# A four-layer graph network: where the eight tile transposes of the third layer stand among the gather matmuls

## The chip, the cores and the metric

The kernel runs on one core of one Trainium2 chip. The metric is the device time of one execution in microseconds (us), the median of a few runs. On the core work five engines that this text names as the profile does: PE (TensorE, matmuls; its weight loads are shown apart as PEld), DVE (VectorE), ACT (ScalarE), POOL (GpSimd) and SP (SyncE, which here only issues transfers). They run side by side and meet at semaphores.

## The reference, cut to what matters

Four layers over 4096 nodes with 64 features and one 4096 x 4096 weighted adjacency matrix. Each layer normalises its input, aggregates over neighbours and adds to x. The change touches the third layer only (index 2), a hyperbolic one:

```python
def _logmap(x, y, c):
    sub = _mobius_add(-x, y, c)
    sub_norm = jnp.maximum(jnp.linalg.norm(sub, axis=-1, keepdims=True), MIN_NORM)
    ...
    arg = jnp.clip(sqrt_c * sub_norm, 0.0, TANH_CLIP)
    return 2.0 / (sqrt_c * lam_x) * jnp.arctanh(arg) * sub / sub_norm

deg = jnp.maximum(adj.sum(axis=1, keepdims=True), 1e-08)
log_ij = _logmap(x[:, None, :], x[None, :, :], c)
agg = jnp.einsum('ij,ijc->ic', adj / deg, log_ij)
```

So for every pair (i, j) there is one scalar, a function of the distance of the two nodes, which is symmetric in i and j; it is multiplied by adj[i, j] and the product gathers the features of j into i.

## The kernel before

**Units.** The third layer walks over the upper half of the pair matrix. A strip S is 512 nodes wide (eight strips), a pair p is 2 x 128 nodes. A unit is one (S, p) block of 256 x 512 scalars, held as 128 x 1024. Strip S has the units p = 2S to 15, so there are 16 + 14 + ... + 2 = 72 units. The first two units of a strip lie on the diagonal; the other units, 56 of them, are "mirrored": since the scalar is symmetric, their transpose serves the block below the diagonal too.

**The chain of one unit n**, in the order in which its data flow:

1. PE, `scores2` (L648): two fp32 matmuls (4 records of 512 columns) into one of two pairs of PSUM banks (0-1 or 2-3).
2. ACT, square (L879) of those banks into SBUF; then PE, `sides2` (two bf16 matmuls of 512 columns, shown under L452) adds a second term into the same banks.
3. DVE, `rest2` (L1235); ACT, Ln (L885), Exp (L891), Exp (L892), called `roots2`.
4. DVE, `sum2` (L1241), which needs the Exp of L891 and the sides; ACT, Ln (L896), called `arc2`; DVE, `pair2` (L1247). The result, the matrix of scalars, is in `sum_`, which has three buffers. It signals pair_ready.
5. POOL (L415) multiplies `sum_` with the near adjacency tile in place and signals near_ready.
6. Mirrored units only: PE, `mirror2` (L671), eight 128 x 128 fp32 transposes of `sum_` into PSUM banks 4-5; it signals mirror_ready. DVE, `far2` (L1253), multiplies those banks with the far adjacency tile and signals far_ready.
7. PE, `gather2_near` (fp32, shown under L452): two matmuls of 512 columns, 4 records, into bank 6, where it accumulates over the strip; `gather2_far`: four matmuls of 256 columns, 8 records, into bank 7. DVE, `far2_out` (L1261 or L1263), takes bank 7 out for each mirrored unit and signals far_out; `near2_out` (L1271 or L1274) takes bank 6 out once a strip.

**The order of PE.** It is written out by hand. In step n PE does `scores2(n+1)`, `sides2(n)`, `mirror2(n-1)`, `gather2_near(n-2)`, `gather2_far(n-2)`, each where it exists. So three units are in flight. Before `mirror2(n-1)` it waits for pair_ready of n-1 and for far_ready of the mirrored unit before, which has to have left banks 4-5.

**The order of DVE**, also by hand, in its iteration n: `far2_out(n-3)`, `near2_out(n-3)` where a strip ends, `sum2(n)`, `far2(n-1)`, `rest2(n+1)`, `pair2(n)`. ACT: `roots2(n)`, square(n+1), `arc2(n)`. Each engine does its work strictly in this order.

**SP** loads near and far tiles five units ahead into a ring (the fifth buffer is the tensor H), as soon as the gathers of the unit that had the buffer are done. Both kernels leave this alone.

The diff touches the loop of PE around L700 and the loop of DVE at its end.

Of the kernel before, what the change touches and what calls it, by code (L numbers as in the profile page):

```python
# [21 lines left out]
D = 64  # L22
P = 128
T = N // P
BANK = 512
# [19 lines left out]
ST = STRIP // P  # L45
NS = N // STRIP
PAIR = 2 * P
RING2 = 5
ROT = 2
ROTS = 3  # L50

UNITS = [(S, p) for S in range(NS) for p in range(2 * S, T // 2)]
NU = len(UNITS)


def mirrored(n):
    S, p = UNITS[n]
    return p >= 2 * S + 2


def mirrors(n):

    return sum(mirrored(m) for m in range(n + 1))
# [6 lines left out]
def closes(n):  # L70
    return n == NU - 1 or UNITS[n + 1][0] != UNITS[n][0]
# [11 lines left out]
def graph_layers(nc, x, adj_t, codes, w0_t, b0, w1_t, b1, wq_t, bq, wk_t, bk, scalars, w2, b2, w3, b3, out):  # L83
    ctx = ExitStack()
    with ctx:
        def sb(name, shape, dt=F32):
            return ctx.enter_context(nc.sbuf_tensor(name, shape, dt))
# [3 lines left out]
        def sem(name):  # L91
            if name not in named:
                named[name] = ctx.enter_context(nc.semaphore(name))
            return named[name]
# [9 lines left out]
        PS = ctx.enter_context(nc.psum_tensor("PS", [P, 8 * BANK], F32))  # L104
# [7 lines left out]
        ident = sb("ident", [P, P])  # L112
# [36 lines left out]
        def banks(a, b):  # L149
            return PS[:, a * BANK:b * BANK]  # L150
# [15 lines left out]
        def units_of(first, n):  # L166
            return work[:, first * UNIT:(first + n) * UNIT].rearrange("p (k n) -> p k n", k=n)
        root, lnr, sum_ = units_of(0, ROT), units_of(2, ROT), units_of(4, ROTS)
        GA = work[:, 7 * UNIT:11 * UNIT]
        Zn = work[:, 11 * UNIT:11 * UNIT + T * ROWS].rearrange("p (t c) -> p t c", t=T)  # L170
# [4 lines left out]
        def near(n):  # L175
            k = n % RING2
            return ring[:, k, 0:UNIT] if k < RING else Hflat[:, 0:UNIT]

        def far(n):
            k = n % RING2  # L180
            return ring[:, k, UNIT:2 * UNIT] if k < RING else Hflat[:, UNIT:2 * UNIT]

        def z_banks(n):
            return banks(ROT * (n % ROT), ROT * (n % ROT) + 2)
# [14 lines left out]
        def agg2_col(t):  # L199

            g, t = t // TG, t % TG
            return (2 + 3 * g + t // 7) * BANK + (t % 7) * (D + 1)
# [244 lines left out]
        def _(pe):  # L447
            mm = nc.tensor.matmul

            def add(out_ap, lhsT, rhs, starts=False):  # L450

                return mm(out_ap, lhsT, rhs, start=starts, stop=True, skip_group_check=True)  # L452
# [184 lines left out]
            def scores2(n):  # L637
                S, p = UNITS[n]
                if n == 0:
                    pe.wait_ge(sem("zr_out_a"), 1)  # L640
                    pe.wait_ge(sem("zl_out_a"), 1)
                if n == 2:
                    pe.wait_ge(sem("zr_out_v"), 1)
                    pe.wait_ge(sem("zl_out_v"), 1)
                if n >= ROT:
                    pe.wait_ge(sem("sum_ready"), n - ROT + 1)
                for q in range(2):
                    ins = mm(z_banks(n)[:, q * BANK:(q + 1) * BANK], TA[0:D + 1, (2 * p + q) * P:(2 * p + q + 1) * P],  # L648
                             TB[0:D + 1, S * STRIP:(S + 1) * STRIP], start=True, stop=True)
                ins.then_inc(sem("z_ready"), 1)  # L650

            def sides2(n):
                S, p = UNITS[n]
                pe.wait_ge(sem("square_ready"), n + 1)
                if n == 0:
                    pe.wait_ge(sem("kap_ready"), 4)
                for q in range(2):
                    ins = add(z_banks(n)[:, q * BANK:(q + 1) * BANK], kap_l[0:ROWS, (2 * p + q) * P:(2 * p + q + 1) * P],
                              kap_r[0:ROWS, S * STRIP:(S + 1) * STRIP])
                ins.then_inc(sem("side_ready"), 1)  # L660

            def mirror2(n):
                pe.wait_ge(sem("pair_ready"), n + 1)
                if n == 2:
                    pe.wait_ge(sem("zr_out_v"), 1)
                if mirrors(n) > 1:
                    pe.wait_ge(sem("far_ready"), mirrors(n) - 1)
                for i in range(ST):
                    for q in range(2):
                        c = 4 * BANK + i * PAIR + q * P  # L670
                        ins = nc.tensor.transpose(PS[:, c:c + P], sum_[:, n % ROTS, q * BANK + i * P:q * BANK + (i + 1) * P], ident[:, :])  # L671
                ins.then_inc(sem("mirror_ready"), 1)

            def gather2_near(n):
                S, p = UNITS[n]
                pe.wait_ge(sem("near_ready"), n + 1)
                if opens(n) and n:
                    pe.wait_ge(sem("near_out"), S)
                for q in range(2):
                    ins = add(PS[0:D + 1, 6 * BANK:7 * BANK], Zn[:, 2 * p + q, 0:D + 1], near(n)[:, q * BANK:(q + 1) * BANK],  # L680
                              opens(n) and q == 0)
                ins.then_inc(sem("agg2_near"), 1)

            def gather2_far(n):
                S, p = UNITS[n]
                pe.wait_ge(sem("far_ready"), mirrors(n))
                if mirrors(n) > 1:
                    pe.wait_ge(sem("far_out"), mirrors(n) - 1)
                for i in range(ST):
                    ins = add(PS[0:D + 1, 7 * BANK:7 * BANK + PAIR], Zn[:, S * ST + i, 0:D + 1], far(n)[:, i * PAIR:(i + 1) * PAIR], i == 0)  # L690
                ins.then_inc(sem("agg2_far"), 1)

            def nodes2(first, end):
                for t in range(first, end):
                    ins = mm(PS[:, agg2_col(t):agg2_col(t) + D + 1], GA[0:D + 1, t * P:(t + 1) * P], ident[0:D + 1, 0:D + 1],  # L695
                             start=True, stop=True)
                ins.then_inc(sem("agg2_nodes"), 1)

            scores2(0)
            for n in range(NU + 2):  # L700
                if n + 1 < NU:
                    scores2(n + 1)
                if n < NU:
                    sides2(n)
                if 1 <= n <= NU and mirrored(n - 1):
                    mirror2(n - 1)
                if n >= 2:
                    gather2_near(n - 2)
                    if mirrored(n - 2):
                        gather2_far(n - 2)  # L710
# [247 lines left out]
        def _(dve):  # L958
# [279 lines left out]
            def sum2(n):  # L1238
                dve.wait_ge(sem("root_ready"), n + 1)
                dve.wait_ge(sem("side_ready"), n + 1)  # L1240
                V.scalar_tensor_tensor(sum_[:, n % ROTS, :], z_banks(n), 1.0, sum_[:, n % ROTS, :], ALU.max, ALU.add)\  # L1241
                 .then_inc(sem("sum_ready"), 1)

            def pair2(n):
                dve.wait_ge(sem("tau_ready"), n + 1)
                dve.wait_ge(sem("rin_ready"), n + 1)
                V.scalar_tensor_tensor(sum_[:, n % ROTS, :], sum_[:, n % ROTS, :], TAU_MAX, lnr[:, n % ROT, :], ALU.min, ALU.mult)\  # L1247
                 .then_inc(sem("pair_ready"), 1)

            def far2(n):  # L1250
                dve.wait_ge(sem("mirror_ready"), mirrors(n))
                dve.wait_ge(sem(f"far_loaded{n % RING2}"), 16 * sum(mirrored(m) for m in range(n % RING2, n + 1, RING2)))
                V.tensor_tensor(far(n), banks(4, 6), far(n), ALU.mult).then_inc(sem("far_ready"), 1)  # L1253

            def far2_out(n):
                S, p = UNITS[n]
                at = GA[0:D + 1, p * PAIR:(p + 1) * PAIR]
                got = PS[0:D + 1, 7 * BANK:7 * BANK + PAIR]
                dve.wait_ge(sem("agg2_far"), mirrors(n))
                if S == 0:  # L1260
                    V.tensor_copy(at, got).then_inc(sem("far_out"), 1)  # L1261
                else:
                    V.tensor_tensor(at, at, got, ALU.add).then_inc(sem("far_out"), 1)  # L1263
# [13 lines left out]
            for n in range(NU + 3):  # L1277
                if n >= 3 and mirrored(n - 3):
                    far2_out(n - 3)
                if n >= 3 and closes(n - 3):  # L1280
                    near2_out(n - 3)
                if n < NU:
                    sum2(n)
                if 1 <= n <= NU and mirrored(n - 1):
                    far2(n - 1)
                if n + 1 < NU:
                    rest2(n + 1)
                if n < NU:
                    pair2(n)

            link(V.reciprocal(agg_y[:, :], deg[:, :]))
            link(V.tensor_tensor(agg_y[:, :], agg_y[:, :], iball[:, :], ALU.mult))
# [105 lines left out]
```

## Time and profile before

| what | value |
|---|---|
| median of 3 runs | 1236.74 us (1235.92 to 1241.49) |
| the profiled execution, its own time | 1238.63 us |
| its span in the trace | 1236.9 us, so 1.7 us lie around it |
| PE busy | 1100.3 us, 89% of the span |
| DVE busy | 857.2 us, 69% |
| ACT busy | 767.2 us, 62% |
| POOL busy | 371.0 us, 30% |
| third layer, the unit loop | about 630 to 1079 us of the span |

A line of a timeline gives the start of a group of like instructions, the time from the first start to the last end, engine, line and operation, output and input, shapes, their count, and in brackets the idle time before it with what ended that. Matmuls overlap: the record of one lasts past the start of the next, so what a group occupies on PE is read from its start to the start of the next group. An fp32 matmul is two records. "PEclk" is the share of the full TensorE clock that was granted.

### The profile page before, as it was taken

To read this page: it belongs to the slowest core of one execution; us is meant where nothing else is said; L and a number is where in the kernel's file an instruction comes from. 1 tells how busy PE (TensorE), PEld (TensorE's weight loads), DVE (VectorE), ACT (ScalarE), POOL (GpSimd) and SP (SyncE) were. 2 spreads that over 40 slices of the span, in tenths; PEclk is the share of its full clock that TensorE was granted. 3 is DMA by queue.
4 is the path that set the end of the run, shared out by engine and by line. 5 is a ranking of instruction groups with operands and counts; after the bars stand their busy time and mean duration, and the time that the engine had idled before them with its cause. 6 is when DMAs were issued, how large, how long until landed. Compare 5 with 4: busy or idle time off the path is not lost.

```text
span 1236.9 us, 15886 instructions
## 1 busy us (share of the span) xinstructions
PE 1100.3 (89%) x5064; PEld 495.1 (40%) x5084; DVE 857.2 (69%) x916; ACT 767.2 (62%) x780; POOL 371.0 (30%) x279
## 2 busy tenths in 40 slices
PE   2799999997599999999349999999999999954997
PEld 0233333347422222222124554554545454443555
DVE  7799989964766666666746777677677777666553
ACT  2355555543556656666338778778787888634864
POOL 6434334320100000000154334334333434323533
PEclk9899999996799999999768999999999999966999
DMA  8899999950067887776303446446454545111653
GB/s 321 282 349 366 341 338 354 343 205 1 1 229 260 265 267 268 266 261 219 136 1 121 156 133 192 158 127 202 138 170 136 179 131 163 52 55 43 194 185 89
DMA packets 96285, 237.97 MB, mean 192 GB/s; under 512 B 16368, under 2 KB 45040, under 8 KB 79856
## 3 DMA queue, kind: packets, MB, share of 16 engines
q1 hardware_dynamic: 87024, 220.62, 53.6%
q10 hardware_dynamic: 9216, 16.78, 3.5%
q8 instruction: 25, 0.41, 0.1%
q14 instruction: 20, 0.16, 0.0%
HBM read 219.55 MB, written 17.83 MB: 192 GB/s over the span
## 4 chain that ended last, share of the span: by engine, by line
PE 83%; DVE 7%; POOL 3%; issue 3%; ACT 2%; DMA 1%; SPq 0%; POOLq 0%; DVEq 0%; ACTq 0%
PE PS L452 55%; PE PS L648 10%; PE PS L595 6%; PE PS L596 4%; PE PS L671 4%; PE PS L484 1%; PE PS L462 1%; PE PS L474 1%; DVE st L1023 1%; DVE work L1020 1%; PE PS L695 1%; POOL work L408 1%; ACT work L765 1%; POOL X L401 1%; POOL brow L375 1%
## 5 line engine op out<-in xcount | busy, mean ns | idle before, releaser
L1160 DVE TENSOR_TENSOR work<-work,ring 128x1024 f32<-128x1024 f32 x128 | 157.1, 1228 | 99.4 <-ACT work L857 99.4
L857 ACT ACTIVATE work<-PS,att_sc 128x1024 f32<-128x1024 f32 x128 | 154.1, 1205 | 98.7 <-PE PS L596 98.4
L800 ACT ACTIVATE work<-PS 128x1024 uint8<-128x1024 f32 x128 | 124.1, 1021 | 130.0 <-PE PS L452 130.0
L452 PE MATMUL PS<-work,ystage 128*64 128x512 f32 x768 | 200.7, 616 | 0.9 <-DVE work L1160 0.9
L415 POOL TENSOR_TENSOR ring<-work,ring 128x1024 f32<-128x1024 f32 x58 | 137.3, 2366 | 213.1 <-DVE work L1247 213.1
L452 PE MATMUL PS<-ring,work 128*65 128x256 f32 (+1 forms) x568 | 184.2, 471 | 2.6 <-DVE work L1274 2.6
L1241 DVE SCALAR_TENSOR_TENSOR work<-PS,work 128x1024 f32<-128x1024 f32 x72 | 88.2, 1225 | 119.5 <-PE PS L452 106.3
L648 PE MATMUL PS<-TB,TA 65*128 65x512 f32 x288 | 139.2, 606 | 4.2 <-DVE work L1241 2.9
L381 POOL COPY ystage<-H 128x64 f32 x60 | 83.2, 1387 | 135.9 <-PE PS L452 135.5
L452 PEld LDWEIGHTS PS<-ring,work 128*65 128x65 f32 x568 | 77.6, 139 | 86.0 <-issue 64.4
L896 ACT ACTIVATE work<-work 128x1024 f32<-128x1024 f32 x72 | 76.0, 1055 | 45.3 <-DVE work L1241 45.1
L595 PE MATMUL PS<-work 128*128 128x512 f16 x256 | 98.8, 386 | 4.9 <-DVE work L1032 3.1
L596 PE MATMUL PS<-work 128*128 128x512 f16 x256 | 97.4, 380 | 0.0
L885 ACT ACTIVATE work<-work 128x1024 f32<-128x1024 f32 x72 | 75.9, 1054 | 32.9 <-DVE work L1235 32.9
L1247 DVE SCALAR_TENSOR_TENSOR work<-work 128x1024 f32<-128x1024 f32 x72 | 87.8, 1219 | 9.0 <-ACT work L896 9.0
L452 PE MATMUL PS<-work,sstage 128*64 128x512 bf16 x768 | 86.3, 388 | 7.1 <-DVE work L1344 5.0
L452 PE MATMUL PS<-ring,ystage 128*64 128x512 f32 x256 | 65.1, 631 | 30.4 <-POOL ystage L365 19.1
L396 POOL COPY ystage<-work 128x64 f32 x30 | 7.1, 238 | 249.1 <-PE PS L452 249.1
L934 ACT ACTIVATE work<-ring 128x1024 int16<-128x1024 uint8 x64 | 66.5, 1054 | 22.6 <-PE PS L452 15.3
L891 ACT ACTIVATE work<-work 128x1024 f32<-128x1024 f32 x72 | 76.1, 1057 | 2.3
L648 PEld LDWEIGHTS PS<-TB,TA 65*128 65x128 f32 x288 | 55.2, 193 | 55.8 <-issue 42.8
L452 PEld LDWEIGHTS PS<-work,ystage 128*64 128x64 f32 x768 | 41.0, 135 | 87.7 <-issue 73.2
(203 smaller groups left out, 1641.4 us busy)
## 6 DMA issues: line engine op xcount, KB each, us to landing
ring<-in_adj_t SPq DMA_DIRECT2D x96, 1024.0 KB, 5.1
ring<-in_adj_t SPq DMA_DIRECT2D x100, 512.0 KB, 3.7
work<-in_adj_t SPq DMA_DIRECT2D x32, 1024.0 KB, 7.6
codes<-work ACTq DMA_DIRECT2D x64, 256.0 KB, 6.3
ring<-codes SPq DMA_DIRECT2D x64, 256.0 KB, 3.1
H<-in_adj_t SPq DMA_DIRECT2D x28, 512.0 KB, 4.5
X<-in_x SPq DMA_DIRECT2D x2, 512.0 KB, 5.3
out_x<-X SPq DMA_DIRECT2D x2, 512.0 KB, 4.0
```

Source lines behind the costliest of these rows:

```text
L381: nc.gpsimd.tensor_copy(ystage[:, k, 0:D], H[:, jt, :]).then_inc(sem("staged0"), 1)
L415: nc.gpsimd.tensor_tensor(near(n), sum_[:, n % ROTS, :], near(n), ALU.mult).then_inc(sem("near_ready"), 1)
L452: return mm(out_ap, lhsT, rhs, start=starts, stop=True, skip_group_check=True)
L595: mm(o, k_hl[:, bass.ts(jt, P)], q_hh[:, i0:i0 + BANK], start=True, stop=False)
L596: ins = mm(o, k_hl[:, bass.ts(jt, P)], q_ll[:, i0:i0 + BANK], start=False, stop=True)
L648: ins = mm(z_banks(n)[:, q * BANK:(q + 1) * BANK], TA[0:D + 1, (2 * p + q) * P:(2 * p + q + 1) * P], TB[0:D + 1, S * STRIP:(S + 1) * STRIP ...
L800: nc.scalar.activation(made[:, k, u * UNIT:(u + 1) * UNIT], PS[:, (4 + 2 * u) * BANK:(6 + 2 * u) * BANK], ACT.Relu).then_inc(sem("codes_ma ...
L857: nc.scalar.activation(att[:, u % 2, :], PS[:, b * BANK:(b + 2) * BANK], ACT.Sigmoid, bias=att_sc[:, 2:3], scale=att_sc[:, 1:2]).then_inc( ...
L891: nc.scalar.activation(sum_[:, n % ROTS, :], lnr[:, n % ROT, :], ACT.Exp, scale=0.5).then_inc(sem("root_ready"), 1)
L1160: V.tensor_tensor(prob[:, u, :], att[:, u % 2, :], ring[:, s, (u % 2) * UNIT:(u % 2 + 1) * UNIT], ALU.mult)\
L1241: V.scalar_tensor_tensor(sum_[:, n % ROTS, :], z_banks(n), 1.0, sum_[:, n % ROTS, :], ALU.max, ALU.add)\
L1247: V.scalar_tensor_tensor(sum_[:, n % ROTS, :], sum_[:, n % ROTS, :], TAU_MAX, lnr[:, n % ROT, :], ALU.min, ALU.mult)\
```

## The change

In PE's loop, wherever the unit n-1 and the unit n-2 are both mirrored (49 of the 56 mirrored units; the other seven are the first mirrored unit of each strip), the block of eight transposes of n-1 and the gathers of n-2 are replaced by `mirror_and_gather2(n-1)`: transpose, gather, transpose, gather, and so on. The first four gather instructions are those of the far tile, the last four those of the near tile, which now take 256 columns each in place of 512 (four in place of two). All the waits of the transposes and of both gathers are taken at its start. mirror_ready is signalled by the last of the eight transposes. On DVE, `far2(n-1)` moves from behind `sum2(n)` to the end of the iteration, behind `rest2(n+1)` and `pair2(n)`, for all 56 mirrored units.

```diff
+            def mirror_and_gather2(n):
+                S, p = UNITS[n - 1]
+                pe.wait_ge(sem("pair_ready"), n + 1)
+                pe.wait_ge(sem("far_ready"), mirrors(n) - 1)
+                pe.wait_ge(sem("far_out"), mirrors(n) - 2)
+                pe.wait_ge(sem("near_ready"), n)
+                for k in range(2 * ST):
+                    i, q = k // 2, k % 2
+                    c = 4 * BANK + i * PAIR + q * P
+                    turned = nc.tensor.transpose(PS[:, c:c + P], sum_[:, n % ROTS, q * BANK + i * P:q * BANK + (i + 1) * P], ident[:, :])
+                    if k < ST:
+                        far_done = add(PS[0:D + 1, 7 * BANK:7 * BANK + PAIR], Zn[:, S * ST + k, 0:D + 1],
+                                       far(n - 1)[:, k * PAIR:(k + 1) * PAIR], k == 0)
+                        if k == ST - 1:
+                            far_done.then_inc(sem("agg2_far"), 1)
+                    else:
+                        q, half = (k - ST) // 2, (k - ST) % 2
+                        near_done = add(PS[0:D + 1, 6 * BANK + half * PAIR:6 * BANK + (half + 1) * PAIR], Zn[:, 2 * p + q, 0:D + 1],
+                                        near(n - 1)[:, q * BANK + half * PAIR:q * BANK + (half + 1) * PAIR])
+                turned.then_inc(sem("mirror_ready"), 1)
+                near_done.then_inc(sem("agg2_near"), 1)
...
                 if n < NU:
                     sides2(n)
+                if 2 <= n <= NU and mirrored(n - 1) and mirrored(n - 2):
+                    mirror_and_gather2(n - 1)
+                    continue
                 if 1 <= n <= NU and mirrored(n - 1):
                     mirror2(n - 1)
...
                 if n < NU:
                     sum2(n)
-                if 1 <= n <= NU and mirrored(n - 1):
-                    far2(n - 1)
                 if n + 1 < NU:
                     rest2(n + 1)
                 if n < NU:
                     pair2(n)
+                if 1 <= n <= NU and mirrored(n - 1):
+                    far2(n - 1)
```

## Rows read from the trace of the kernel before

**Rows 1.** The page, part 4: the chain that ended last, shares by engine.

```profile
PE 83%; DVE 7%; POOL 3%; issue 3%; ACT 2%; DMA 1%; SPq 0%; POOLq 0%; DVEq 0%; ACTq 0%
```

**Rows 2.** Busy time by stage: columns stretch, length, PE, PEld, DVE, ACT, POOL, PEclk, DMA.

```profile
150.00:152.00 2.00, 0.83 (x5) 0.30 (x5) 1.73 (x3) 1.74 (x2) 0.56 (x1) 1.00 1.02 251
...
638.00:659.00 21.00, 12.40 (x17) 4.00 (x18) 7.92 (x8) 11.23 (x12) 10.29 (x4) 0.51 0.00 0
...
659.00:1065.00 406.00, 406.00 (x1560) 209.54 (x1559) 288.64 (x318) 337.02 (x339) 160.03 (x68) 1.00 0.49 156
```

**Rows 3.** Timeline of PE over one mirrored unit in the steady state.

```profile
801.57 1.88 PE L648 MATMUL PS<-TB,TA 65*128 65x512 f32 x4
...
803.29 0.60 PE L452 MATMUL PS<-work 67*128 67x512 bf16 x2
...
803.73 1.04 PE L671 MATMUL PS<-ident,work 128*128 128x128 f32 x8
...
804.60 3.61 PE L452 MATMUL PS<-H,work 128*65 128x512 f32 x12
...
808.04 1.88 PE L648 MATMUL PS<-TB,TA 65*128 65x512 f32 x4
```

**Rows 4.** Timeline of DVE and POOL around the same unit.

```profile
804.00 1.23 DVE L1241 SCALAR_TENSOR_TENSOR work<-PS,work 128x1024 f32<-128x1024 f32 x1 [1.80 <-PE PS L452]
...
805.14 1.21 DVE L1253 TENSOR_TENSOR ring<-PS,ring 128x1024 f32<-128x1024 f32 x1
...
806.87 1.22 DVE L1247 SCALAR_TENSOR_TENSOR work<-work 128x1024 f32<-128x1024 f32 x1
...
808.16 2.37 POOL L415 TENSOR_TENSOR ring<-work,ring 128x1024 f32<-128x1024 f32 x1 [4.11 <-DVE work L1247]
...
808.24 0.42 DVE L1263 TENSOR_TENSOR work<-work,PS 65x256 f32<-65x256 f32 x1 [0.16 <-PE PS L452]
```

**Rows 5.** Waits, 659 to 1065 us: who waited for whom, us in total, times, longest.

```profile
PEld PS L671 <- DVE work L1247: 4.7, 12, 0.4
```

**Rows 6.** Timeline of PE where strip 1 begins: its first two mirrored units.

```profile
759.95 1.09 PE L671 MATMUL PS<-ident,work 128*128 128x128 f32 x8
...
764.85 1.09 PE L671 MATMUL PS<-ident,work 128*128 128x128 f32 x8
```

**Rows 7.** Timeline of DVE and ACT over the same stretch.

```profile
760.70 1.22 DVE L1241 SCALAR_TENSOR_TENSOR work<-PS,work 128x1024 f32<-128x1024 f32 x1 [0.81 <-ACT work L891]
...
761.84 1.21 DVE L1253 TENSOR_TENSOR ring<-PS,ring 128x1024 f32<-128x1024 f32 x1
...
762.43 1.05 ACT L896 ACTIVATE work<-work 128x1024 f32<-128x1024 f32 x1
...
763.57 1.22 DVE L1247 SCALAR_TENSOR_TENSOR work<-work 128x1024 f32<-128x1024 f32 x1
```

**Rows 8.** Timeline of PE and ACT where strip 0 begins.

```profile
663.12 1.06 ACT L896 ACTIVATE work<-work 128x1024 f32<-128x1024 f32 x1
...
666.33 1.04 PE L671 MATMUL PS<-ident,work 128*128 128x128 f32 x8
```

**Rows 9.** Timeline of PE and DVE at the end of the unit loop.

```profile
1063.57 1.09 PE L671 MATMUL PS<-ident,work 128*128 128x128 f32 x8
...
1069.76 1.23 DVE L1241 SCALAR_TENSOR_TENSOR work<-PS,work 128x1024 f32<-128x1024 f32 x1 [0.75 <-ACT work L891]
```

**Rows 10.** Timeline of PE: other transposes, whose stationary operand has 67 columns.

```profile
628.20 0.93 PE L630 MATMUL PS<-ident,work 128*67 128x128 f32 x7
```

**Rows 11.** Groups of weight loads, whole kernel: count, busy us, mean ns, idle before.

```profile
L452 PEld LDWEIGHTS PS<-ring,work 128*65 128x65 f32 x568 | 77.6, 139 | 86.0 <-issue 64.4
...
L671 PEld LDWEIGHTS PS<-ident,work 128*128 128x128 f32 x448 | 51.4, 140 | 13.4 <-DVE work L1247 4.7
```

**Rows 12.** Timeline of PE: a gap of the first layer at full clock.

```profile
151.79 1.51 PE L452 MATMUL PS<-ring,ystage 128*64 128x512 f32 x6 [1.17 <-ACT work L800]
```

## The prediction

> **What bounds the kernel now.** I read the page's chain first: PE carries 83% of it [rows 1]. Then the busy time by stage [rows 2]: from 659 to 1065 us, nearly the whole unit loop of the third layer, PE is busy 406.00 of 406.00 us at full clock, while DVE has 289, ACT 337 and POOL 160. "Busy" could still hide waits, so the next view is the timeline of one unit [rows 3]. Read from start to start, scores take 1.72 us (801.57 to 803.29), sides 0.44, the eight transposes 0.87, the twelve gather records 3.44, together 6.47 us. Each piece is streaming alone: 1.72 over 4 records of 512 columns is 0.43; the four near records, 512 columns too, take the same, which leaves 1.72 for the eight far records of 256 columns, 0.215 each, half of 0.43; a transpose is 0.109, half of that again, for its 128 columns. There is no hole to close. The waits say the same: what PE loses ahead of the transposes is 4.7 us over 12 cases [rows 5], and part of that is covered by running matmuls; all 12 are the first two mirrored units of strips 1 to 6. The other 44 blocks have no wait at all. So an interleave has nothing on PE to hide, and what it delays decides.
>
> **The steady unit, 42 of the 49 changed steps.** I set t = 0 where the scores begin. Before, transposes stand at 2.16 to 3.03 and DVE's far2 follows sum2 at once (805.14, t = 3.57), then rest2, pair2 (806.87) [rows 4]. After, one transpose and its gather take 0.109 + 0.43 = 0.54, the eighth transpose starts at 2.16 + 7 x 0.54 = 5.94. The nearest rows for its way to DVE: sum2 starts 0.71 after the first of two sides records (803.29 to 804.00), far2_out 0.20 after the end of the gathers (808.04 to 808.24); I take 0.4 after the last transpose's start. far2 then runs from 6.34 for 1.21 and is done at 7.55, far2_out (0.42) at about 7.9. PE wants both before its next transposes, at 6.47 + 2.16 = 8.63. Margins 1.0 and 0.7 us. pair2 no longer stands behind far2; it needs ACT's Ln, which follows sum2, and ends by 6.0, ahead of the last transpose, so the moved far2 blocks nothing: the next sum2 waits for sides at 8.9 anyway. near_ready (POOL starts 1.29 after pair2 and takes 2.37 [rows 4]) is asked for almost a unit later. Cost of the longer wait list: 0. The far tile's transfer is five units ahead, and buffers come free at the end of the gathers as before: 0. If this cover were gone, DVE would have to be 0.7 us later than I read.
>
> **The start of a strip: a new wait.** Here two steps are short, since diagonal units have no transposes or far gathers, and ACT and DVE are late. The first mirrored unit of a strip (call it a) is transposed as a block at 759.95, the second (b) at 764.85 [rows 6], right behind pair2 of b, 763.57 + 1.22 = 764.79, so 0.06 from DVE to PE [rows 7]. In the kernel before, far2 of a lies at 761.84, in DVE's time while ACT does the Ln (762.43 + 1.05 = 763.48). After, this slot is idle, pair2 of b cannot move up (it needs that Ln: 763.51 at best), and far2 of a comes behind it: 763.51 + 1.14 (spacing of DVE instructions, 760.70 to 761.84) = 764.65, done 765.86, PE goes on at 765.93. It has to, since the transposes of b overwrite the banks that far2 of a reads. That is 765.93 - 764.85 = 1.08 us later, and behind it stands everything of PE: transposes and, now in the same sequence, the gathers of a. PE is the bound in the units that follow, so nothing gives it back. Strips 1 to 5 have the same pattern: 5 x 1.08 = 5.40.
>
> Strip 0 starts with PE late (clock 0.51 to 659 us [rows 2]): ACT's Ln ends at 664.18, pair2 at 664.20, far2 at 665.34, PE could go at 665.34 + 1.21 + 0.06 = 666.61 against 666.33 [rows 8]: 0.28.
>
> Strip 6 is followed by the end of the loop. The step loses 1.08 as well, but then sum2 of the last unit, at 1069.76 and held by ACT [rows 9], starts the chain that ends the loop. After: the transposes of the last mirrored unit start at 1063.57 + 1.08 = 1064.65, the eighth at 1068.43, far2 at 1068.83, far2_out 1.14 later, 1069.97, and sum2 0.34 behind that, 1070.31, since DVE takes them in this order. So 0.55, which reaches the last gathers through pair2 and near2_out.
>
> Sum of the waits: 5.40 + 0.28 + 0.55 = 6.23 us.
>
> **The interleave itself.** Two more near instructions: eight records at 0.215 for four at 0.43, at most 0.02 a unit. Switching between transposes and gathers: the trace has one change each way per unit, now eight. From the last transpose to the gather: 0.87 over eight is 0.109 for each, the last included, so 0. From sides to the transposes: 0.44 for two records of 0.43 together, at most 0.01. No row shows an fp32 gather followed by a transpose, nor a gather whose load stands under a transpose while another such pair follows. Bounds: 0 and 0.01 for each of 14 added changes, so with the near split 0 to 0.16 a unit, 0 to 7.8 us over 49. I take 0.03 a unit, near the lower end, since the rows of one kind and the other agree with pure streaming: 1.5 us. A gain here would need a transpose below 0.109. The seven other transposes of [rows 10], with 67 stationary columns in place of 128, have the same spacing, (0.93 - 0.27)/6 = 0.11, where 0.27 is one record (1.04 less 7 x 0.11 [rows 3]); so the spacing goes by the 128 streamed columns, and not by the load.
>
> The Trainium skill, page "TensorE: Matmul & The Clock Gate", section "Back-to-back issue gap", says that the spacing of matmuls in a stream of loads and matmuls is set by both and gives about 81 ns for 128 columns. If a transposition were held by its load, hiding the load beneath a gather would pay; by that page's figure it would be 28 ns for each of 392, 11 us. The rows speak against it, as said.
>
> **The sum.** 6.23 + 1.5 = 7.7 us. On the profiled execution: 1238.6 + 7.7 = 1246.3. That run is 1.9 above the median of the three, and I give a median: 1236.7 + 7.7 = **1244.4**. Its own range, with the runs' spread and the switching bounds, is 1241 to 1250.
>
> **Rivals.**
> (a) *The wait is handed back.* At the first two mirrored units of a strip sum2 waited for ACT (0.81 us at 760.70 [rows 7]), so ACT is late there; if ACT rather than PE sets the pace for the units behind, PE's 1.08 us is time that it would have waited anyway. It decides if ACT's lateness lasts past unit b. What is left is the interleave: 1236.7 + 1.5 = 1238.2, not slower. Against: the waits ahead of the transposes stop after b [rows 5], and PE is full from there on.
> (b) *Loads exposed.* A gather's load stands under a transpose of 0.109, while a load lasts 0.139 in the lines of the trace [rows 11]. If the 0.03 showed, 392 x 0.03 = 12 us more: 1256. It decides from a load over 0.109 long. Against: transposes follow each other at 0.109 with loads of 0.140 [rows 11].
> (c) *The clock.* PE now stands still for about 1.1 us more at a strip's start; if the clock fell to half there, as it was for 21 us from 638 [rows 2], even 8 us at half would cost 4 each time: 6 x 4 more, 1268. Against: a gap of 1.17 us in the first layer left the clock at 1.00 [rows 2, 12], and the gap here is about 1.2 with the 0.1 of before.
> (d) *DVE too late in each unit.* mirror_ready comes over 0.7 later than read, so PE waits for far2_out: from there each 0.1 us costs 42 x 0.1 = 4.2 us; with 0.2 it is 1253.
> (e) *Faster: the transposes cost less than their block.* If their 0.109 were a load's time and the stream half of it, 0.055 x 392 = 21 us less, with the waits 1222. Rows 10 speak against it.
> (f) The order does not do what it says, say the transposes don't run between the gathers because PE keeps waiting: the far margin of (d), no other case.
>
> **How the numbers follow.** Forecast 64%, (a) 14%, (b) 8%, (c) 3%, (d) 6%, (e) 5%. The range leaves out (e), (c), half of (b) and of (d) and of (a) less: 1238 to 1253. What a measurement can tell from no change is 0.5%, 6.2 us, so 1242.9 is the line. A fifth of the forecast's own spread lies under it, about 13%, with (a) that makes 27% same; slower 68%, faster 5%.
>
> **What would show it.** Right: in the waits, PE ahead of L671 released by DVE L1253 (far2) in place of L1247, six times with about 1 us; a steady unit of 6.48 to 6.52; DVE's far2 starting about 6.3 into the unit; a loop 7 to 8 us longer; the clock 1.00 until the loop's end. Wrong: a steady unit above 6.6 (b or d), below 6.4 (e), the clock under 1 in the loop (c), or strips whose second mirrored unit waits no longer than before (a).

## The result and the profile after

| | before | changed |
|---|---|---|
| median of 20 runs | 1236.59 us (1235.43 to 1241.59) | 1243.05 us (1241.47 to 1251.93) |
| the profiled execution, its span | 1238.63, 1236.9 us | 1251.21, 1249.2 us |

The medians differ by 6.5 us, where 7.7 was forecast. The ratio is 1.0062 with a 95% interval of 1.0044 to 1.0081; that is the ratio of the means, 7.7 us apart, which hold the upper runs of both kernels. The runs of the changed kernel fall into two groups, 14 from 1241.5 to 1243.7 and 6 from 1251.1 to 1251.9, and the profiled one is of the upper group. What the upper group has more is told below.

The page after, engines' busy time: PE has 196 more matmul records, the two added near instructions (two records each) of 49 units.

```profile
PE 1106.5 (89%) x5260; PEld 526.0 (42%) x5280; DVE 863.7 (69%) x916; ACT 766.5 (61%) x780; POOL 370.7 (30%) x279
```

The waits from 659 to 1072 us, in the columns of [rows 5]. L703 is a transpose of the interleave, L671 one of the seven blocks that are left, L1279 is far2, L1267 sum2, L1273 pair2, L1289 far2_out (the added lines move the numbers).

```profile
PE PS L703 <- issue: 5.5, 6, 1.1
...
PEld PS L671 <- DVE work L1273: 2.2, 6, 0.4
...
DVE ring L1279 <- PE PS L703: 14.1, 37, 2.2
```

PE stands still ahead of L703 six times, 5.5 us in all: the starts of strip 0 (0.2) and of strips 1 to 5 (1.06 each); strip 6's lies behind this stretch. The releaser is given as "issue": where four waits are taken at one point the trace does not name the one that ended last. Before, [rows 5] named pair2 there. far2 now waits for the last transpose of its unit, 37 times in this line, which costs PE nothing by itself.

**A steady unit**, against [rows 3, 4]: timeline of the changed kernel around one unit.

```profile
803.46 1.88 PE L648 MATMUL PS<-TB,TA 65*128 65x512 f32 x4
...
805.61 0.27 PE L703 MATMUL PS<-ident,work 128*128 128x128 f32 x1
...
805.72 0.59 PE L452 MATMUL PS<-H,work 128*65 128x256 f32 x2
...
809.40 0.27 PE L703 MATMUL PS<-ident,work 128*128 128x128 f32 x1
...
809.71 1.22 DVE L1279 TENSOR_TENSOR ring<-PS,ring 128x1024 f32<-128x1024 f32 x1 [0.25 <-PE PS L703]
...
809.94 1.88 PE L648 MATMUL PS<-TB,TA 65*128 65x512 f32 x4
...
810.85 0.41 DVE L1289 TENSOR_TENSOR work<-work,PS 65x256 f32<-65x256 f32 x1
```

The unit runs from 803.46 to 809.94, 6.48 us for 6.47. Its last transpose starts 5.94 into it, far2 at 6.25 and far2_out is done at 810.85 + 0.41, 7.80 into it, 0.8 ahead of PE's next transposes at 8.63. There is no wait of PE in the unit.

**The start of strip 1**, against [rows 6, 7]: timelines of PE, DVE and ACT of the changed kernel.

```profile
760.68 1.09 PE L671 MATMUL PS<-ident,work 128*128 128x128 f32 x8
...
765.05 0.60 PE L452 MATMUL PS<-work 67*128 67x512 bf16 x2
...
766.70 0.30 PE L703 MATMUL PS<-ident,work 128*128 128x128 f32 x1 [1.06 <-issue]
```

```profile
761.44 1.23 DVE L1267 SCALAR_TENSOR_TENSOR work<-PS,work 128x1024 f32<-128x1024 f32 x1 [0.81 <-ACT work L917]
...
764.24 1.23 DVE L1273 SCALAR_TENSOR_TENSOR work<-work 128x1024 f32<-128x1024 f32 x1 [0.25 <-ACT work L922]
...
765.38 1.22 DVE L1279 TENSOR_TENSOR ring<-PS,ring 128x1024 f32<-128x1024 f32 x1
```

```profile
763.16 1.05 ACT L922 ACTIVATE work<-work 128x1024 f32<-128x1024 f32 x1
```

ACT's Ln ends at 764.21, pair2 starts at 764.24, far2 of the first mirrored unit 1.14 behind it, at 765.38, and ends at 766.60; the first transpose of the second unit starts at 766.70. From the block of the first unit to the first transpose of the second it was 4.90 us (759.95 to 764.85 in [rows 6]) and is 6.02 here.

**The end of the loop**, against [rows 9]: the scores of the last unit and the last near gathers, in the kernel before and in the changed one, with DVE of the changed one.

```profile
1061.32 1.88 PE L648 MATMUL PS<-TB,TA 65*128 65x512 f32 x4
...
1074.60 5.32 PE L452 MATMUL PS<-ring,work 128*65 128x512 f32 x8 [2.61 <-DVE work L1274]
```

```profile
1071.21 1.88 PE L648 MATMUL PS<-TB,TA 65*128 65x512 f32 x4
...
1085.00 5.32 PE L452 MATMUL PS<-ring,work 128*65 128x512 f32 x8 [2.02 <-DVE work L1300]
```

```profile
1078.71 1.22 DVE L1279 TENSOR_TENSOR H<-PS,H 128x1024 f32<-128x1024 f32 x1 [0.52 <-PE PS L703]
...
1080.18 1.21 DVE L1267 SCALAR_TENSOR_TENSOR work<-PS,work 128x1024 f32<-128x1024 f32 x1
```

From those scores to the last near gathers it was 13.28 us and is 13.79, 0.51 more. sum2 of the last unit comes 8.97 us behind the scores where it came 8.44 behind them (1069.76 in [rows 9]), since far2 and far2_out stand ahead of it and far2 waits for the last transpose.

**Where the time went.** I compare the starts of the scores of each unit in the two traces. The distance grows by 0.37 us at strip 0, by 1.10 at each of strips 1, 3 and 5, by 2.79 and 2.78 at strips 2 and 4, by 0.01 in each of the other steps that interleave, and by nothing elsewhere; the 0.51 of the end come on top. The surplus at strips 2 and 4, 1.69 each, is a clock matter, as the busy time by stage around the start of strip 2 shows (columns as in [rows 2]; the eighth figure is PEclk):

```profile
846.80:850.20 3.40, 3.40 (x16) 1.68 (x15) 1.96 (x3) 3.37 (x5) 2.37 (x1) 1.00 0.87 288
...
850.20:853.60 3.40, 2.34 (x8) 0.82 (x7) 3.15 (x4) 3.37 (x4) 1.23 (x1) 1.00 0.64 194
...
853.60:857.00 3.40, 3.40 (x11) 2.21 (x12) 2.75 (x3) 3.37 (x5) 1.14 (x1) 0.50 0.35 120
...
857.00:860.40 3.40, 3.40 (x17) 2.23 (x16) 1.20 (x2) 1.85 (x2) 2.36 (x1) 1.00 0.00 0
```

In the second stretch PE stood still for 1.1 us (2.34 busy of 3.40); the next 3.4 us ran at half clock, and then it was full again. Strips 1, 3 and 5 had the same wait and kept their clock. The other traces, below, show how often that came in them.

### The profile page after: what moved, and what is told of

The parts are those of the page before. It is cut to its first block, busy times and chain, and to the rows that moved or that the text cites. A ratio compares the mean times of both kernels' runs of the same rounds, so it can differ in the third digit from the quotient of the medians.

```text
span 1249.2 us, 16279 instructions
## 1 busy us (share of the span) xinstructions
PE 1106.5 (89%) x5260; PEld 526.0 (42%) x5280; DVE 863.7 (69%) x916; ACT 766.5 (61%) x780; POOL 370.7 (30%) x279
## 4 chain that ended last, share of the span: by engine, by line
PE 83%; DVE 7%; POOL 3%; issue 3%; ACT 2%; DMA 1%; SPq 0%; POOLq 0%; DVEq 0%; ACTq 0%
PE PS L452 56%; PE PS L648 10%; PE PS L595 5%; PE PS L596 4%; PE PS L703 4%; PE PS L484 1%; PE PS L462 1%; PE PS L474 1%; DVE st L1049 1%; DVE work L1046 1%; POOL work L408 1%; PE PS L718 1%; ACT work L791 1%; PE PS L671 1%; POOL X L401 1%
## 5 line engine op out<-in xcount | busy, mean ns | idle before, releaser
L452 PE MATMUL PS<-ring,work 128*65 128x256 f32 (+1 forms) x720 | 215.2, 409 | 2.0 <-DVE work L1300 2.0
L1267 DVE SCALAR_TENSOR_TENSOR work<-PS,work 128x1024 f32<-128x1024 f32 x72 | 88.1, 1224 | 80.1 <-PE PS L452 75.2
L648 PE MATMUL PS<-TB,TA 65*128 65x512 f32 x288 | 139.2, 606 | 4.2 <-DVE work L1267 2.9
L703 PE MATMUL PS<-ident,work 128*128 128x128 f32 x392 | 108.1, 276 | 6.5 <-issue 6.5
L1273 DVE SCALAR_TENSOR_TENSOR work<-work 128x1024 f32<-128x1024 f32 x72 | 88.2, 1225 | 34.6 <-ACT work L922 34.6
L452 PEld LDWEIGHTS PS<-ring,work 128*65 128x65 f32 x720 | 91.8, 140 | 46.2 <-issue 20.1
L922 ACT ACTIVATE work<-work 128x1024 f32<-128x1024 f32 x72 | 76.0, 1055 | 50.6 <-DVE work L1267 50.6
L905 ACT ACTIVATE work<-PS 128x1024 f32<-128x1024 f32 x72 | 73.2, 1017 | 39.6 <-PE PS L648 39.6
L648 PEld LDWEIGHTS PS<-TB,TA 65*128 65x128 f32 x288 | 55.3, 193 | 55.7 <-issue 42.8
```

The costliest lines, as they stand in the source:

```text
L703: turned = nc.tensor.transpose(PS[:, c:c + P], sum_[:, n % ROTS, q * BANK + i * P:q * BANK + (i + 1) * P], ident[:, :])
```

## The experiments

The gauge for the loop, used throughout, leaves out what happens ahead of it: the time from the start of the scores of unit 5 (L648, 664.18 in the first trace) to the start of the last near gathers (1074.60). It is 410.42 us in that trace, and 410.41 to 410.43 in the four further traces of the kernel before, so it resolves 0.1 us where the medians resolve some 3.

| kernel | loop gauge, us | against before | half-clock stretches in it | without them |
|---|---|---|---|---|
| before (5 traces) | 410.42 | 0 | 0 | 0 |
| changed, first trace | 420.56 | +10.14 | 2 | +6.8 |
| changed, after_again | 417.20 | +6.78 | 0 | +6.8 |
| e1_order_only | 419.91 | +9.49 | 2 | +6.1 |
| e2_first_early | 412.41 | +1.99 | 0 | +2.0 |
| e3_interleave_only | 482.98 | +72.56 | 8 | +59.0 |
| e4_longer_wait | 433.83 | +23.41 | 5 | +15.0 |
| e5_near_first | 410.40 | -0.02 | 0 | 0.0 |
| e6_block_near_first, e6_again | 409.13 | -1.29 | 0 | -1.3 |

A stretch is 3.4 us long and counts 1.69 us in the last column.

**e1_order_only: DVE's order alone.** The kernel before, with

```diff
-                if 1 <= n <= NU and mirrored(n - 1):
-                    far2(n - 1)
                 if n + 1 < NU:
                     rest2(n + 1)
                 if n < NU:
                     pair2(n)
+                if 1 <= n <= NU and mirrored(n - 1):
+                    far2(n - 1)
```

> The kernel before with one part of the change alone: DVE's far2 stands at the end of the iteration, the transposes stay a block of eight. Theory (the loss is the wait of the second mirrored unit of each strip for far2 of the first): the whole loss of the waits is here, 0.37 at strip 0, 1.10 at each of the strips 1 to 5 and about 0.5 at the end, 6.4 us, and steady units stay at 6.47 us; about 1242.5 us against 1236.6. Rival A (the interleave is what costs): as before, 1236.6. Rival B (half-clock stretches in the loop come from PE's waits): the trace or some of the runs show stretches at half clock here too, worth 1.7 us each, and some runs stand several us above the rest.

Measured: 1247.23 us (1243.48 to 1248.29, 6 runs), ratio 1.0073, interval 1.0049 to 1.0097. The block of transposes still stands, and so its wait has a name here. PE at the start of strip 1:

```profile
766.93 1.06 PE L671 MATMUL PS<-ident,work 128*128 128x128 f32 x8 [1.10 <-DVE ring L1253]
...
765.57 1.22 DVE L1253 TENSOR_TENSOR ring<-PS,ring 128x1024 f32<-128x1024 f32 x1
```

1.10 us, released by far2. The loss is there with no interleave at all, so rival A falls. Rival B holds: the trace has half-clock stretches at 853.9 and 990.4, behind the waits of strips 2 and 4, the same two as in the changed kernel. That this kernel's runs stand no lower than the changed one's (lowest 1243.5 against 1241.5) was not expected and is not explained; its loop without the stretches is 0.7 shorter. Most of that is the end of the loop, where 0.5 was expected here and 0.03 is lost: the 0.51 of the changed kernel takes the late far2 and the interleaved transposes together.

**e2_first_early: the interleave alone.** The changed kernel, with far2 of a strip's first mirrored unit in its old place:

```diff
+                first_of_strip = 2 <= n <= NU and mirrored(n - 1) and not mirrored(n - 2)
+                if first_of_strip:
+                    far2(n - 1)
                 if n + 1 < NU:
                     rest2(n + 1)
                 if n < NU:
                     pair2(n)
-                if 1 <= n <= NU and mirrored(n - 1):
+                if 1 <= n <= NU and mirrored(n - 1) and not first_of_strip:
                     far2(n - 1)
```

> The changed kernel with the transposes interleaved as in the change, but DVE's far2 of the first mirrored unit of each strip back in its old place behind sum2; all other far2 stay late. Theory: the wait of 1.22 us ahead of the second mirrored unit falls back to the old 0.16, the interleave alone costs 0.01 us for each of 49 units, 0.5 us: 1237.1 us, no stretch at half clock in the loop. Rival A (the interleave costs): about 1243, with the loop as long as in the changed kernel.

Measured: 1238.72 us (1237.39 to 1240.29, 12 runs), ratio 1.0006, interval 0.9991 to 1.0021; the loop 2.0 longer, not 0.5. The wait of 1.1 is gone, but 0.27 a strip is left, one unit later. PE and DVE at the third mirrored unit of strip 1:

```profile
770.32 1.22 DVE L1273 SCALAR_TENSOR_TENSOR work<-work 128x1024 f32<-128x1024 f32 x1 [0.25 <-ACT work L922]
...
771.47 1.22 DVE L1279 TENSOR_TENSOR H<-PS,H 128x1024 f32<-128x1024 f32 x1
...
772.60 0.41 DVE L1289 TENSOR_TENSOR work<-work,PS 65x256 f32<-65x256 f32 x1
...
773.26 0.30 PE L703 MATMUL PS<-ident,work 128*128 128x128 f32 x1
```

ACT is still late there, so pair2 (770.32) is, and far2 of the second unit and far2_out of the first stand behind it. PE, which asks for far2_out ahead of its transposes, starts them at 773.26, 0.25 behind far2_out's end and 0.23 late. The interleave itself, in all the steps away from strip starts, is 0.01.

**e3_interleave_only: the transposes of the change with DVE's order of before.** The diff is the change without its DVE part.

> The changed kernel with DVE's order of before: transposes interleaved, far2 behind sum2 everywhere. Theory: far2 now waits for the last transpose of a unit, about 3 us later than in the block, and rest2, pair2 and far2_out stand behind it; PE then waits for far2_out about 1.0 us in every steady unit and more at strip starts, so the loop grows by some 50 us, 1285 to 1295, with half-clock stretches on top if waits bring them. Rival (far2's place does not matter in the steady unit): 1243.

Measured: 1313.19 us. The steady unit is 7.67 us, 1.20 more, where I had put 1.0. PE and DVE in one:

```profile
796.94 1.22 DVE L1279 TENSOR_TENSOR ring<-PS,ring 128x1024 f32<-128x1024 f32 x1 [2.40 <-PE PS L703]
...
798.09 0.68 DVE L1261 TENSOR_SCALAR work<-work 128x1024 f32<-128x1024 f32 x1
...
798.68 1.22 DVE L1273 SCALAR_TENSOR_TENSOR work<-work 128x1024 f32<-128x1024 f32 x1
...
799.82 0.41 DVE L1289 TENSOR_TENSOR work<-work,PS 65x256 f32<-65x256 f32 x1
...
800.49 0.30 PE L703 MATMUL PS<-ident,work 128*128 128x128 f32 x1 [1.00 <-DVE work L1289]
```

far2 at 796.94 has waited 2.40 us for the last transpose, rest2 and pair2 stand behind it, far2_out behind these (799.82), and PE's next transposes, at 800.49, have waited 1.00 for it. Its idle time is counted from the end of the record of the sides before it, which lasts 0.17 past its place in the stream (0.60 for two records 0.43 apart), hence 1.0 of idle time and 1.20 a unit. 42 steady units of 1.20 are 50 of the 59 us; strip starts and the end of the loop have the rest. So the move of far2 is what the interleave needs, and it is right in the steady unit; the eight half-clock stretches add 13.5.

**e4_longer_wait: the suspected wait made longer.** The changed kernel, with

```diff
                 if 1 <= n <= NU and mirrored(n - 1):
+                    if not mirrored(n - 2):
+                        V.tensor_tensor(sqr[:, 0:16, :], sqr[:, 16:32, :], sqr[:, 16:32, :], ALU.mult)
                     far2(n - 1)
```

> The changed kernel with one more DVE instruction of 128x1024 fp32 (its result is used by nobody) ahead of far2 of the first mirrored unit of each strip. Theory: the wait there grows from 1.22 by about 1.15 to 1.2 us in each of seven strips (less in the last), 7 to 8 us: the lower runs at about 1250 against 1242.5 for those of the changed kernel. If half-clock stretches come from the wait, they get more with a longer one: more than two of the seven starts in the trace, 1.7 us each. Rival (ACT or another engine sets the pace there): less than 3 us.

Measured: 1264.02 us (1263.02 to 1266.01, 5 runs), ratio 1.0198, interval 1.0177 to 1.0218. PE at the start of strip 1, and the added DVE instruction:

```profile
767.11 1.22 DVE L1316 TENSOR_TENSOR work<-work 128x1024 f32<-128x1024 f32 x1
...
769.57 0.30 PE L703 MATMUL PS<-ident,work 128*128 128x128 f32 x1 [2.20 <-issue]
```

The wait is 2.20 for 1.06 in the lines, 1.14 more, and the loop without the stretches grows by 8.2: seven times 1.14, so DVE's instruction falls on the path whole. Five of the seven starts now have a half-clock stretch, where the shorter wait had two or none. The runs lie above the 1250 that was expected for the lower ones; in the traced one the five stretches are 8.5 us of the loop, and 4 us more than in the lower run of the changed kernel lie behind the loop.

**e5_near_first: the wait covered.** The changed kernel, with one step a strip altered in PE's order:

```diff
+                if 3 <= n <= NU and mirrored(n - 1) and mirrored(n - 2) and not mirrored(n - 3):
+                    gather2_near(n - 2)
+                    mirror2(n - 1)
+                    gather2_far(n - 2)
+                    continue
```

> The changed kernel, with one step per strip altered: in the step of the second mirrored unit PE does the near gather of the first unit (1.72 us), then the block of eight transposes, then the far gather; far2 stays late everywhere. Theory: the wait for far2 of the first unit, 1.22 us, is covered by the near gather, and also the 0.16 us behind pair2; what is left is the interleave of 42 units, 0.4 us: about 1236.5, no half-clock stretch in the loop. Rival (something else at the strip's start sets the time, say ACT): PE waits at another place of that step, and the time stays near 1243.

Measured: 1235.94 us (1234.90 to 1241.82, 12 runs), ratio 0.9995, interval 0.998 to 1.001. PE at the start of strip 1:

```profile
765.02 0.60 PE L452 MATMUL PS<-work 67*128 67x512 bf16 x2
...
765.46 1.88 PE L452 MATMUL PS<-ring,work 128*65 128x512 f32 x4
...
767.18 1.04 PE L671 MATMUL PS<-ident,work 128*128 128x128 f32 x8
...
765.36 1.22 DVE L1284 TENSOR_TENSOR ring<-PS,ring 128x1024 f32<-128x1024 f32 x1
```

The near gather runs from 765.46 to 767.18 while far2 (765.36, for 1.22) is at work; the transposes follow without a hole. The loop is as long as before's: the gain at the block of the second unit, 0.155 a strip, and 0.09 at the end of the loop pay for the interleave and for a delay of 0.09 one unit later. This is the cleanest test: 42 units are still interleaved, far2 is still late everywhere, and the loss is gone.

**e6_block_near_first and e6_again: a version without the interleave.** The kernel before, with PE's near gather ahead of the block in the steps of the first two mirrored units of a strip, and far2 of these two late:

```diff
+                early = 3 <= n <= NU and mirrored(n - 1) and not mirrored(n - 3)
+                if early:
+                    gather2_near(n - 2)
                 if 1 <= n <= NU and mirrored(n - 1):
                     mirror2(n - 1)
                 if n >= 2:
-                    gather2_near(n - 2)
+                    if not early:
+                        gather2_near(n - 2)
...
+                late = 3 <= n <= NU and mirrored(n - 1) and not mirrored(n - 3)
-                if 1 <= n <= NU and mirrored(n - 1):
+                if 1 <= n <= NU and mirrored(n - 1) and not late:
                     far2(n - 1)
...
+                if late:
+                    far2(n - 1)
```

> The kernel before with its block of transposes, and in the steps of the first two mirrored units of each strip the near gather ahead of the block and far2 of these two units late on DVE. Theory: the 0.16 us that PE lost twice a strip behind pair2 are covered: 12 x 0.155 = 1.9 us less than before, 1234.7. Rival: the waits move to another place of the same steps (sum2 and ACT are late there too), and the time stays at 1236.6.

> The kernel with the block of transposes and the near gather first in two steps a strip, again, for a closer comparison with before: its trace has a loop 1.3 us shorter than before's (0.155 and 0.085 us at six strip starts). 1235 us against 1236.3, a ratio of 0.999 if before's upper runs are left out of the thought, down to 0.996 with them. Rival: no difference, 1.000.

Measured: 1235.28 us (8 runs), ratio 0.9967, interval 0.9950 to 0.9984, and again 1234.88 us (1233.64 to 1236.48, 12 runs), ratio 0.9974, interval 0.9961 to 0.9988. It beats both kernels, by little. 1.3 us of that is the loop, in two steps of a strip, 0.155 and 0.085, where 1.9 was expected; much of the rest of the ratio comes from the upper runs of the kernel before, 7 of the 13 that the first ratio is taken against, of which these 20 runs have none; that was not traced to the change.

**after_again and before_again: a second trace of each.**

> The changed kernel itself, for a second trace and more times beside before's on one chip. Theory: the waits and the 0.01 us a unit are in each execution, and the stretches at half clock behind a wait are in some only: with them 8 us stand between the runs. A second trace has the same waits of 1.22 us at six strip starts; compared at the same mean clock (0.944 against 0.943) the kernel is 6.5 to 7 us behind before. Rival: the distance of the groups has another cause, and a trace of a fast execution has the two stretches at half clock in the loop as well.

> The kernel before itself, for a second trace. Theory: no stretch at half clock inside the unit loop, its twelve waits are 0.16 us each; what separates its own runs (1235 to 1242) lies ahead of the loop or behind it. Rival: its waits too bring half-clock stretches in the loop.

Measured: the changed kernel 1243.59 us (1241.61 to 1251.59, 10 runs), ratio 1.0064, interval 1.0040 to 1.0088; again in two groups. This trace is of the lower group, and the start of strip 2 has the same wait with no half clock behind it:

```profile
852.00:855.40 3.40, 2.35 (x13) 1.47 (x12) 3.00 (x4) 3.40 (x4) 2.38 (x1) 1.00 0.85 264
...
855.40:858.80 3.40, 3.40 (x17) 2.23 (x16) 2.63 (x4) 3.37 (x4) 1.65 (x1) 1.00 0.00 0
```

PE is busy 2.35 of 3.40, as in the first trace, and the clock stays at 1.00. Its loop is 6.78 longer than before's. The second trace of the kernel before is of a run of 1234.63 us, with no half-clock stretch in its loop, as expected; the spans of the two second traces differ by 1240.5 - 1232.9 = 7.6. Between the two traces of the changed kernel 8.7 us lie (1249.2 - 1240.5): 3.4 in the loop, its two stretches, and 5.2 behind it, since from the last near gathers to the end it is 164.2 and 158.9. Only the upper one has a half-clock stretch at 1085.7, right behind those gathers' wait, and one in the fourth layer, at 1208.6. Which of the equal waits the clock falls behind, and in which execution, is not explained.

**before_3, before_4, before_5: an upper run of the kernel before.**

> The kernel before once more, to catch in a trace one of its upper executions (some 1241 us; four in ten lie there, and none of 20 of the version with the near gather first). If a trace falls there: theory A (its own waits of 0.16 us can also bring half-clock stretches in the unit loop) shows stretches at half clock between 659 and 1065 us; theory B (they have nothing to do with the loop) shows a loop like the other traces' and the 5 us elsewhere.

before_4 and before_5 had the same expectation. Measured: 1236.42, 1240.49 and 1236.69 us. before_4 is the upper one, and its loop is 410.42 like the others', with no half clock: theory A falls. From its last near gathers to its end it is 164.1 us, in before_3 and before_5 158.5, in the first trace 162.3. What it has alone of the five traces is a half-clock stretch in the fourth layer. PE there, and the busy time by stage:

```profile
1196.93 6.41 PE L452 MATMUL PS<-work,sstage 128*64 128x512 bf16 x42 [2.20 <-ACT work L934]
```

```profile
1195.00:1198.50 3.50, 1.57 (x14) 0.94 (x16) 2.07 (x4) 2.44 (x3) 0.27 (x1) 0.96 0.98 317
...
1198.50:1202.00 3.50, 3.50 (x21) 1.70 (x19) 2.01 (x3) 3.39 (x4) 1.35 (x2) 0.56 1.01 378
```

A wait of 2.20 us for ACT, then 3.4 us at half clock from 1198.2. The same wait stands in before_3 with the clock left at full:

```profile
1194.50 8.87 PE L452 MATMUL PS<-work,sstage 128*64 128x512 bf16 x80 [2.14 <-ACT work L934]
```

It is there in all five traces, 2.09 to 2.20 us; the half clock behind it is in one. Against the first trace of this kernel, whose loop and head are alike, that stretch is 1.8 of the 1.9 us between the spans (1238.8 and 1236.9). Those two have a half-clock stretch at 1075.3 too, right behind the wait of the last near gathers, which the other three lack. So what the upper run of the kernel before has more lies behind the loop, as does the larger part of what the upper run of the changed kernel has more; what makes the clock fall behind the same wait in some executions only stays open.

## Why the prediction was right, point by point

- **PE is the bound and has no hole**: right. The interleave found nothing to fill: a transpose still takes 0.11 to the gather behind it (805.61 to 805.72 above).
- **The steady unit costs nothing on DVE**: right. far2 was put at 6.34, it is at 6.25; the margin for far2_out was put at 0.7, it is 0.8. e3 shows what stands without that order.
- **The new wait at strip starts**: right in place, mechanism and size: 1.08 forecast, 1.10 measured, at strips 1 to 5; strip 0 has 0.37 for 0.28. For the end of the loop 0.55 was forecast, with sum2 of the last unit held behind far2_out; 0.51 was measured, by that way. The waits' sum is 6.4 for 6.23. e1 has the wait without the interleave, e5 the interleave without the wait.
- **The interleave itself**: the one term mis-sized. 0.03 a unit was taken, 0.01 measured, 0.5 us in all for 1.5. 0.01 is what the near split costs by the mean spacing of the records, eight of 0.2158 for four of 0.429; the change of kind costs nothing that shows.
- **The sum**: 6.8 us in the loop without half-clock stretches for 7.7, nearly all of the difference from the interleave's term. In the run profiled first the loop is 10.1 longer, outside the "7 to 8 us" that was to show it right, and the clock does fall in the loop, which was named as a sign of being wrong.
- **Rival (c), the clock**: given 3% and wrongly weighed. The row that spoke against it was a single wait that left the clock at full. It does fall behind some of these waits, in the execution first traced, of the group that holds six of 20 runs; the price in my text, 4 us for each of six starts, was too high: it was 1.69 for each of two. The median stays with the group whose traced run has none, and that is luck: nothing in the forecast spoke for it. A median in the upper group, near 1251, would have been some 14.6 above before, nearly twice the 7.7. That the means lie 7.7 apart is luck too, since they hold stretches which the forecast left out.
- **Rival (a)**, handed back: no; the distance stays once it is there. **(b)** and **(e)**: no, loads of 0.14 stay hidden both ways. **(d)**: no.
- The waits were to name far2 as what releases the transposes, six times with about 1 us: the size and the places are right, the name is "issue"; e1 names far2.

## What to carry to other kernels

Where an engine streams without a hole, another order of the same instructions has nothing to fill, and its price lies in what it delays; look for that price where the steady pattern breaks (here the start of a strip), not in the steady unit, which had 0.8 us to spare. Moving one DVE instruction behind two others cost 6 of the 6.8 us, and putting 1.7 us of ready PE work in front of the wait took it all back. A gauge between two instructions of the trace, the same in five executions to 0.02 us, tells what a median with a spread of 6 us can't.

## What the runs showed of the hardware

- A wait of PE of 1.1 us, in a loop that is otherwise full, was followed by 3.4 us at half clock (1.2 GHz) at two of six places (the starts of strips 1 to 6) in one execution and at none in another of the same kernel; in e1 it was two of six again. Waits of 2.2 us had it at five of six in the one trace of e4, whose strip 0, with 1.3, had none. Each stretch cost 1.69 us. In the loop of e3, with 1.0 us of idle time in each of 42 steady units of 7.67 us, it came eight times.
- In e4 the added DVE instruction has both operands and its result in SBUF, and POOL's multiply that ran beside it took 3.28 us, against 2.37 elsewhere:

```profile
767.27 3.28 POOL L415 TENSOR_TENSOR H<-work,H 128x1024 f32<-128x1024 f32 x1 [2.47 <-DVE work L1273]
...
762.43 2.38 POOL L415 TENSOR_TENSOR ring<-work,ring 128x1024 f32<-128x1024 f32 x1 [3.24 <-DVE work L1273]
```

It is 3.27 to 3.29 at all seven places. far2, which reads PSUM, runs beside the same POOL multiply in e1 and in the changed kernel and leaves it at 2.36 to 2.39. Which operand makes the difference was not tried.
